# Biases of the query, key and value projection: from a matmul in each product to a shift of the weights

## The reference

```
x = x + attn(layernorm(x))        # 32 heads, 8 key/value heads, rope, causal, a sink per head
    qkv = n @ qkv_w.T + qkv_b     # 256 -> 3072
    ... softmax(q k / 8, with sink) @ v
    out @ out_w.T + out_b         # 2048 -> 256
x = x + xattn(layernorm(x), ctx)  # 8 heads over slices of the token axis
x = x + ffn(layernorm(x))         # top-1 of 8 experts, and a shared expert
```

## Time and profile before

| | us |
|---|---|
| median of 3 runs | 2182.62 |
| lowest and highest | 2179.29, 2183.5 |
| the profiled execution | 2175.44 |
| its span | 2173.4 |
| PE busy | 1990.2 (92%) |
| DVE busy | 1172.4 (54%) |
| ACT busy | 775.8 (36%) |
| POOL busy | 614.6 (28%) |
| granted clock of PE, mean | 0.978 |

### The profile page before, as it was taken

How to read it: one execution, slowest core, us unless ns; L and a number is a source line. 1 busy time by engine, 2 the same in 40 slices (tenths; PEclk the granted TensorE clock), 3 DMA queues, 4 the chain that set the end, 5 groups by cost and what they waited for, 6 DMA issues and landing times. The chain is left out here.

```text
span 2173.4 us, 49370 instructions
## 1 busy us (share of the span) xinstructions
PE 1990.2 (92%) x17680; PEld 1484.0 (68%) x17681; DVE 1172.4 (54%) x2333; ACT 775.8 (36%) x1463; POOL 614.6 (28%) x1100
## 2 busy tenths in 40 slices
PE   4999999999999999997799999999999599999998
PEld 3877787778777877786566666666666355666665
DVE  6566556655665566555566566666666122222221
ACT  3333333333333333333245444445455211211211
POOL 2232223222322232222222333332332310014443
PEclk9999999999999999999799999999999799999999
DMA  4011111111111111111323323323222155222221
GB/s 160 26 50 37 48 36 48 36 48 36 48 36 48 36 48 36 48 33 52 94 57 81 83 59 81 79 63 81 74 68 66 39 173 185 70 66 66 66 64 43
DMA packets 123545, 139.65 MB, mean 64 GB/s; under 512 B 16706, under 2 KB 118086, under 8 KB 121642
## 3 DMA queue, kind: packets, MB, share of 16 engines
q1 hardware_dynamic: 117674, 123.95, 20.3%
q0 software_dynamic: 5760, 14.06, 2.0%
HBM read 85.07 MB, written 53.52 MB: 64 GB/s over the span
## 5 line engine op out<-in xcount | busy, mean ns | idle before, releaser
L1032 ACT ACTIVATE xe<-bankXT 128x512 f32<-128x512 f32 x512 | 289.2, 596 | 324.8 <-PE bankXT L1173 317.8
L1073 DVE TENSOR_REDUCE xmax<-bankX 128x4 f32<-128x1024 f32 x256 | 309.2, 1210 | 133.5 <-PE bankX L1162 133.5
L1162 PE MATMUL bankX<-stk,stq 96*128 96x256 f32 x1024 | 230.7, 311 | 24.0 <-DMA rw<-in_rw 10.2
L543 DVE TENSOR_TENSOR oTl<-bankV,oTh 128x512 fp32r<-128x512 f32 x128 | 88.5, 691 | 303.9 <-ACT oTh L431 303.9
L1173 PE MATMUL bankXT<-stq,stk 98*128 98x256 f32 x1024 | 220.5, 298 | 6.7 <-ACT xe L1032 2.8
L1162 PEld LDWEIGHTS bankX<-stk,stq 96*128 96x128 f32 x1024 | 162.3, 198 | 55.5 <-issue 32.0
L649 PE MATMUL bankQ<-wqh,xnTh 128*128 128x512 f32 x384 | 188.5, 491 | 0.0
L1472 DVE TENSOR_TENSOR hid<-bankU,gate 128x512 f32<-128x512 f32 x72 | 49.8, 691 | 245.0 <-PE bankU L1525 241.9
L1173 PEld LDWEIGHTS bankXT<-stq,stk 98*128 98x128 f32 x1024 | 157.4, 191 | 32.0 <-ACT xe L1032 27.6
L360 POOL TENSOR_TENSOR prob<-prob,rden 128x1024 f32<-128x1024 f32 x64 | 121.9, 1905 | 170.5 <-DVE rden L539 170.5
L1188 PE MATMUL bankN<-xe,cT 128*32 128x256 f32 x2048 | 166.2, 397 | 0.2 <-ACT xe L1032 0.2
(11 more groups left out here) (177 smaller groups left out, 4090.2 us busy)
## 6 DMA issues: line engine op xcount, KB each, us to landing
stackk_d<-chl SPq DMA_DIRECT2D x96, 128.0 KB, 2.3
stackq_d<-q2hl SPq DMA_DIRECT2D x96, 128.0 KB, 2.3
stk<-stackk_d SPq DMA_DIRECT2D x32, 384.0 KB
stq<-stackq_d SPq DMA_DIRECT2D x128, 96.0 KB
wexp<-in_wexp SPq DMA_DIRECT2D x8, 1536.0 KB, 8.5
x_d<-x SPq DMA_DIRECT2D x64, 128.0 KB, 2.0
xin<-xg_d SPq DMA_DIRECT2D x40, 128.5 KB, 2.1
x<-in_x SPq DMA_DIRECT2D x32, 128.0 KB, 2.2
```

The lines of the kernel that those rows point to most:

```text
L543: nc.vector.tensor_tensor(oTl[g % 2][:], bV[:, 0, :].rearrange("p (a b) -> p a b", a=4), oTh[g % 2][:].bitcast(F32), ALU.subtract).then_in ...
L1032: nc.scalar.activation(xe[q % 8][:].rearrange("p n m -> p (n m)"), bT[:, q % 2, :], ACT.Exp).then_inc(s_xe, 1)
L1073: nc.vector.tensor_reduce(xmax[tile[1] % 2][:, :, a:b + 1:b - a].rearrange("p m h -> p h m"), bS[:, 2 * (pr % 2):2 * (pr % 2) + 2, :].rear ...
L1162: ins = nc.tensor.matmul(bS[:, q % 4, m * D:(m + 1) * D], stq[p][0:96, hd, m * P:(m + 1) * P], stk[p][0:96, hd // 4, :], start=True, stop= ...
```

## The change

The layer norm has no gain or bias, so each normalised row sums to zero. If 1 is added to each of its 256 entries, the product with a weight column grows by the sum of that column; if a constant is added to the whole weight column, the product with the row plus one grows by 256 times the constant. The weights are shifted by (bias - column sum) / 256, and the product of the row plus one with them is then the old product plus the bias. So no bias matmul is needed in `project`. The bias of the output projection stays a matmul.

- The row plus one: `turn_norm` on ACT uses Identity with bias 1.0 for Copy, and `turn_rest` on DVE a scalar_tensor_tensor (add 1.0, subtract the high part) for a subtraction.
- The column sums are formed on the chip. For each of the three pieces of the projection weight and each half of it, PE forms, in the bank of a product, minus the bias (bf16 matmul with `minusb`) plus the column sum (two float32 matmuls with `onesf`); DVE adds -1/256 of it to the raw weights (`fold`, 128 x 1024 elements, six times). Then ACT makes the high part and DVE the low part, as before.
- The output weights are in a buffer of their own (`stage_o`); their low parts are formed on POOL instead of DVE, and PE waits for them first in tile 1.
- The bias loads, the writes of the terms (two DMAs instead of six) and the read back are issued by ACT, ahead of its other work. SP no longer waits for them.
- Tiles 0 and 1 are normalised before the weights are folded.
- Waits and memsets are moved to fit, and the projection weight is laid out on the host in three pieces of 2 x 1024 columns.

```diff
@@ gpsimd, before the loop
+            for i in range(2):
+                pool.wait_ge(s_hio, i + 1)
+                nc.gpsimd.tensor_tensor(wlo[3 + i], raw[3 + i], whi[3 + i].bitcast(F32),
+                                        ALU.subtract).then_inc(s_loo, 1)
             nc.gpsimd.memset(G.stk0[:].bitcast(F32), 1.0)
@@ scalar
+            act.dma_start(bcol[:, 0:24], A["bqkv"].rearrange("(p c) -> p c", c=24)).then_inc(s_bias, 16)
+            act.dma_start(bcol[:, 24:26], A["bo"].rearrange("(p c) -> p c", c=2)).then_inc(s_bias, 16)
+            act.wait_ge(s_bterm, 1)
+            act.dma_start(G.bias_d[:, 0:3072].rearrange("k (p c) -> p k c", c=24), bterm[:, :, 0:24]).then_inc(s_brow, 16)
+            act.dma_start(G.bias_d[:, 3072:NBIAS].rearrange("k (p c) -> p k c", c=2), bterm[:, :, 24:26]).then_inc(s_brow, 16)
+            act.wait_ge(s_brow, 32)
+            act.wait_ge(s_setb, 1)
+            act.dma_start(bias3[0:3, :], G.bias_d).then_inc(s_brows, 16)
...
-                                     ACT.Copy).then_inc(s_xnTh, 1)
+                                     ACT.Identity, bias=1.0).then_inc(s_xnTh, 1)
...
             turn_norm((0, 0))
+            for i in (0, 1, 3, 2, 4):
+                high(i)
             tiles(act, body)
@@ vector
+            def fold(i, c):
+                dve.wait_ge(s_csum, 2 * i + c + 1)
+                part = raw[i][:, :, c * 512:(c + 1) * 512]
+                nc.vector.scalar_tensor_tensor(part, bk[c][:, 0, :].unsqueeze(1).to_broadcast([P, 2, 512]),
+                                               -1.0 / D, part, ALU.mult, ALU.add).then_inc(s_fold, 1)
+            def low(i):
+                dve.wait_ge(s_hi, i + 1)
+                nc.vector.tensor_tensor(wlo[i], raw[i], whi[i].bitcast(F32), ALU.subtract).then_inc(s_lo, 1)
...
+            stats1((0, 0))
+            norm1((0, 0))
+            stats1((0, 1))
+            turn_rest((0, 0))
+            norm1((0, 1))
...
+            for i in range(2):
+                for c in range(2):
+                    fold(i, c)
+            low(0)
+            for c in range(2):
+                fold(2, c)
+            low(1)
+            low(2)
@@ tensor
-                nc.tensor.matmul(out, onesb[:], bias3[:, col:col + 512], start=True, stop=False)
                 for k in range(2):
                     for n, (a, w) in enumerate(((xnTh, wqh), (xnTh, wql), (xnTl, wqh))):
-                        ins = nc.tensor.matmul(out, a[p][:, k, :], w[:, k, col:col + 512], start=False,
+                        ins = nc.tensor.matmul(out, a[p][:, k, :], w[:, k, col:col + 512], start=(k == 0 and n == 0),
                                                stop=(k == 1 and n == 2))
...
             turn_norm((0, 0))
+            pe.wait_ge(s_brows, 16)
+            pe.wait_ge(s_setb, 2)
+            for i in range(3):
+                pe.wait_ge(s_stage[i], 16)
+                for c in range(2):
+                    need(pe, s_fold, 2 * i + c - 1)
+                    col = i * 1024 + c * 512
+                    nc.tensor.matmul(bk[c][:, 0, :], minusb[:], bias3[:, col:col + 512], start=True, stop=False)
+                    for k in range(2):
+                        ins = nc.tensor.matmul(bk[c][:, 0, :], onesf[:], raw[i][:, k, c * 512:(c + 1) * 512],
+                                               start=False, stop=(k == 1))
+                    ins.then_inc(s_csum, 1)
             pe.wait_ge(s_setv, 1)
-            pe.wait_ge(s_brows, 16)
-            pe.wait_ge(s_lo, NSTAGE)
+            pe.wait_ge(s_setg, 2)
+            pe.wait_ge(s_lo, 3)
             tiles(pe, body)
```

More of the change, by code:

```diff
@@ L176, in attention @@
         NBIAS = 3072 + D
-        with nc.sbuf_tensor("stage", [P, NSTAGE, 2048], F32) as stage, \
+        stage_o = sb("stage_o", [P, 2, 2048])
+        with nc.sbuf_tensor("stage", [P, 3, 2048], F32) as stage, \
+                nc.sbuf_tensor("onesf_a", [P, P], F32) as onesf, \
+                nc.sbuf_tensor("minusb_a", [P, P], BF16) as minusb, \
                 nc.sbuf_tensor("bcol", [P, NBIAS // P], F32) as bcol, \
@@ L191, in attention @@
         s_stage = [sem(f"s_stage{i}") for i in range(NSTAGE)]
-        s_hi, s_lo = sem("s_hi"), sem("s_lo")
-        s_bias, s_setv, s_setg = sem("s_bias"), sem("s_setv"), sem("s_setg")
+        s_hi, s_hio, s_lo, s_loo = sem("s_hi"), sem("s_hio"), sem("s_lo"), sem("s_loo")
+        s_csum, s_fold = sem("s_csum"), sem("s_fold")
+        s_bias, s_setv, s_setg, s_setb = sem("s_bias"), sem("s_setv"), sem("s_setg"), sem("s_setb")
         s_bterm, s_brow, s_brows, c_bias, s_sinks = (
@@ L213, in attention @@
         s_q2hl, s_chl, g_c, g_q2 = sem("s_q2hl"), sem("s_chl"), sem("g_c"), sem("g_q2")
-        whi = [wqh[:].rearrange("p k n -> p (k n)")[:, i * 2048:(i + 1) * 2048] for i in range(3)] + [
+        whi = [wqh[:, :, i * 1024:(i + 1) * 1024] for i in range(3)] + [
             woh[:].rearrange("p k n -> p (k n)")[:, i * 2048:(i + 1) * 2048] for i in range(2)]
-        wlo = [wql[:].rearrange("p k n -> p (k n)")[:, i * 2048:(i + 1) * 2048] for i in range(3)] + [
+        wlo = [wql[:, :, i * 1024:(i + 1) * 1024] for i in range(3)] + [
             wol[:].rearrange("p k n -> p (k n)")[:, i * 2048:(i + 1) * 2048] for i in range(2)]
+        raw = [stage[:, i, :].rearrange("p (k n) -> p k n", k=2) for i in range(3)] + [
+            stage_o[:, i, :] for i in range(2)]
         wsrc = [A["wqkv"][:, i * 2048:(i + 1) * 2048] for i in range(3)] + [
@@ L247, in _ @@
                 sp.dma_start(x[p][:], A["x"][p * P:(p + 1) * P, :]).then_inc(s_x[p], 16)
-            sp.dma_start(bcol[:, 0:24], A["bqkv"].rearrange("(p c) -> p c", c=24)).then_inc(s_bias, 16)
-            sp.dma_start(bcol[:, 24:26], A["bo"].rearrange("(p c) -> p c", c=2)).then_inc(s_bias, 16)
             for i in range(NSTAGE):
-                sp.dma_start(stage[:, i, :], wsrc[i]).then_inc(s_stage[i], 16)
+                sp.dma_start(stage[:, i, :] if i < 3 else stage_o[:, i - 3, :], wsrc[i]).then_inc(s_stage[i], 16)
             sp.dma_start(sinks[:].rearrange("p r s -> p (r s)"),
                          A["sinks"].partition_broadcast(P)).then_inc(s_sinks, 16)
[L255 to L261, removed]
             sp.wait_ge(s_setg, 1)
@@ L313, in _ @@
             nc.gpsimd.memset(G.half[:], 0.5)
+            nc.gpsimd.memset(bias3[:], 0.0).then_inc(s_setb, 1)
+            nc.gpsimd.memset(half_neg[:], -0.5)
+            nc.gpsimd.memset(onesf[:], 1.0)
+            nc.gpsimd.memset(minusb[:], -1.0).then_inc(s_setb, 1)
             pool.wait_ge(s_const, 16)
             nc.gpsimd.tensor_copy(zeros[:, D:D + 1].bitcast(I32), C["none"]).then_inc(s_setg, 1)
-            nc.gpsimd.memset(half_neg[:], -0.5)
             nc.gpsimd.memset(onesb[:], 1.0)
-            nc.gpsimd.memset(bias3[:], 0.0)
             for p in range(2):
@@ L389, in _, with high @@
         def _(act):
-            for i in range(NSTAGE):
-                act.wait_ge(s_stage[i], 16)
-                nc.scalar.activation(whi[i], stage[:, i, :], ACT.Copy).then_inc(s_hi, 1)
+            act.dma_start(bcol[:, 0:24], A["bqkv"].rearrange("(p c) -> p c", c=24)).then_inc(s_bias, 16)
[6 more added lines that the diff above has]
+            act.dma_start(bias3[0:3, :], G.bias_d).then_inc(s_brows, 16)
+            def high(i):
+                if i < 3:
+                    act.wait_ge(s_fold, 2 * i + 2)
+                    nc.scalar.activation(whi[i], raw[i], ACT.Copy).then_inc(s_hi, 1)
+                else:
+                    act.wait_ge(s_stage[i], 16)
+                    nc.scalar.activation(whi[i], raw[i], ACT.Copy).then_inc(s_hio, 1)
             def turn_norm(tile):
@@ L472, in _ @@
         def _(dve):
-            dve.wait_ge(s_const, 16)
-            dve.wait_ge(s_setg, 2)
             def settle(tile):
@@ L501, in turn_rest @@
                 dve.wait_ge(s_xnTh, num(tile) + 1)
-                nc.vector.tensor_tensor(xnTl[tile[1]][:], bO[:, 0, D:2 * D].rearrange("p (k n) -> p k n", k=2),
-                                        xnTh[tile[1]][:].bitcast(F32), ALU.subtract).then_inc(s_xnT, 1)
+                nc.vector.scalar_tensor_tensor(xnTl[tile[1]][:], bO[:, 0, D:2 * D].rearrange("p (k n) -> p k n", k=2),
+                                               1.0, xnTh[tile[1]][:].bitcast(F32), ALU.add,
+                                               ALU.subtract).then_inc(s_xnT, 1)
             def rope(tile, c):
@@ L562, in _ @@
             ch.end()
[L563 to L566, removed]
+            stats1((0, 0))
[3 more added lines that the diff above has]
+            norm1((0, 1))
+            dve.wait_ge(s_const, 16)
+            nc.vector.tensor_copy(identb[:], ident)
+            nc.vector.tensor_copy(maskb[:], C["mask"])
+            nc.vector.tensor_copy(run[:], C["base"]).then_inc(s_setv, 1)
+            for i in range(2):
[6 more added lines that the diff above has]
+            low(2)
+            dve.wait_ge(s_setg, 2)
```

(5 more changed lines are left out.)

4 lines of the change are left out of this document (removed).

## The result

The changed kernel takes 2193.73 us (median of 8, 2189.19 to 2198.83), the kernel before 2180.14 (median of 8): a ratio of 1.0055, with a 95% interval from 1.0041 to 1.0068. By that ratio it is slower by 12 us (the medians lie 13.6 apart), where no measurable change with a lean to faster was forecast, and it lies outside the range. The profiled execution took 2195.25, its span is 2192.9, against 2173.4 before. The profiled execution of the kernel before (2175.44) is 4.7 us under that kernel's median, so spans taken from these two profiles lie further apart than the times do.

A forecast was written before the change was run, and what follows sets the result against it. Up to results(u, 0) DVE's chain with POOL and ACT was taken as the bound, then PE. Start +12.6, tile 0 -2.4, loop -13.3 gave -3.1 us: 2179.5, no measurable change with a lean to faster; range 2172.5 to 2186.

The forecast's parts named there:

- products 0, 1, 2: In the loop before turn_probs(u, 0): PE arrives 0.65 us earlier without their bias matmuls, prob no earlier; gain 0.
- product 3: In the loop between turn_probs(u, 0) and results(u, 0), where PE already waits: gain 0 from its bias matmul.
- Products 4 and 5: In the loop behind the last wait: gain 2 x 0.215, 0.43 us a tile in 31 tiles, 13.3 us.
- The longer stall: PE's wait before turn_probs(u, 0) in the loop: from 1.3 us to 1.7 to 2.0 a tile.
- The cover of product 5: In the loop, DVE's oTl for project_out(u, 2) stays hidden: 0.45 us of room against 0.215.
- Together 2.4: Tile 0 gets 2.4 us shorter: 1.5 for xn, 1.5 for six biases, 0.6 back for the lower clock.
- t0: At the start, the moment when the bias rows are in SBUF: taken as 20 us, bounds 15.9 and 27.7.
- t0 + 20.3: Start of tile 0: 17.3 us of column sums, folds and low parts plus a 3.0 us hold, at 40.3.
- the hold: At the start, POOL's subtraction of the output weights delays DVE's low(1): 3.0 us, bounds 0 and 6.8.
- the second as a rival: At the start, POOL's second subtraction also gets in before low(2): +3.8, giving +0.7 us, 2183.3; chance 0.14.
- The third one: At the start, bias rows no sooner than before, t0 27.7: +4.6 us or more, 2187.2; chance 0.12.
- Rivals 4 and 5: PE is the bound: -29.6, 2153.0, chance 0.05; longer stalls lower PE's clock in each tile: 2216.6, chance 0.05.

The follow-up runs named there:

- e9: The kernel before without the bias matmuls of products 0 to 3 only: 2180.86 us, ratio 0.9995 to the kernel before.
- e10: The kernel before without the bias matmuls of products 4 and 5 only: 2165.73 us, ratio 0.9924 to the kernel before.
- e3: The kernel before without the bias matmul of each product, nothing else changed: 2162.6 us, ratio 0.9921 to the kernel before.
- e2: The changed kernel with POOL's two output-weight subtractions begun only after DVE's three low parts: 2184.4 us, ratio 1.0018 to the kernel before.
- e7: The changed kernel with ACT's first evacuation of the turned probabilities before its second exponential: 2167.85 us, ratio 0.9940 to the kernel before.
- e1: The changed kernel with SP's eight zero writes held back until the bias rows are in SBUF: 2185.3 us, ratio 1.0021 to the kernel before.
- e4: The changed kernel with SP's weight loads and all behind them held back until the bias rows are in SBUF: 2185.89 us, ratio 1.0028.
- e13: The changed kernel with zero writes behind the bias rows and POOL's subtractions behind DVE's low parts: 2177.78 us, ratio 0.9980.
- e8: The changed kernel with one-DMA float32 bias row, POOL's subtractions behind DVE's low parts, and loop reordered on DVE, POOL and ACT: 2117.61 us, ratio 0.9711.
- e14: The changed kernel with one-DMA float32 bias row and POOL's subtractions behind DVE's low parts, loop unchanged: 2165.33 us, ratio 0.9925.
- e5: The changed kernel with the projection bias loaded as one float32 row in one DMA, bf16 terms only for the output bias: 2172.38 us, ratio 0.9957.

## Why the prediction was wrong

- **The loop: right.** "That is 0.43 us a tile in the 31 tiles with a rear part": 0.42 measured. "products 0, 1, 2 [...] Gain 0" and "product 3 [...] Gain 0": e9 measured 0.9995 without all four. Products 4 and 5 carry it all: e10. The number for products 4 and 5 isn't luck: from the last matmul ahead of it to its own end, product 4 takes 0.21 us less in the tiles shown (1.51 instead of 1.72), and from the start of the `results` ahead of it product 5 takes 0.22 less (2.25 instead of 2.47). The longer stall was forecast at 1.7 to 2.0 us and is 1.53, because part of it moved ahead of `turn_probs(u, 0)`, to `turn_qk(tile, 0)` (4.2 us in 24 tiles) and `scores(u, 1)` (2.0 in 11); the wait before `results` grew by about what product 3 lost (0.25). The cover of product 5 held. The changed evacuation on DVE takes 0.41 as before.
- **Tile 0: nearly right, in part by luck.** "Together 2.4": 3.1 up to `turn_norm` of tile 2. e3, e9 and e10 show that this number also depends on when PE's clock rises: there `turn_norm` of tile 2 came 1.0 to 1.6 us later than in the kernel before, from a start at most 0.6 later and with fewer matmuls.
- **The failed step: t0.** "I take 20: the queue is another one, the engines are the same full ones", with an upper bound of 27.7 ("they still wait for the loads"). It was 36.5: the second write was issued at 8.38 instead of 6.5, landed 22.3 us later, and the read back took 5.8 instead of 2.2. The same code had the rows at 35.0 in the profile of e2 and at 33.0 in that of e7, so some 3 us of it vary from one execution to the next; all three are above the bound. Two things stood behind that bound. The first is that the zero writes, which SP no longer holds back, were taken for something that comes after the small writes. They come beside them: between 20 and 31 us the engines are full at 70 GB/s (e1: 9.6 us of t0, with the loads that stand behind the zeros held back too). The second is that the 7.2 us after the loads were taken for the tail of 768 writes alike, where in the changed kernel they are the 4-byte ones: in e1 the 48-byte DMA landed 11.0 us after its issue at 7.62, with the loads, the 4-byte one at 24.5; by themselves they take 2.2 and 9.1 us (e4), and a wait for both DMAs is a wait for the second. In the kernel before the two kinds were issued in turn, and no run separates them there. The upper bound was no bound, since it assumed that nothing else would change on the queues.
- **t0 + 20.3 was t0 + 28.4.** 5.0 of that are the hold: both low parts, 12.6 us against 7.6. I had it at one hold and priced the second as a rival (0.14); the row chosen for it had one POOL operation after another too, and one DVE operation waited for both there. Here DVE got its turn between POOL's two, and each of its own two waited for one (e2). 2.9 are the column sums: 1.93 us from one to the next at the upper clock, where I worked out 1.1. Each float32 matmul of 512 columns stands twice in the trace at 0.43; the group of four in the earlier trace rows belongs to two matmuls of the program. The last 0.2 lie between the end of the last low part and PE's first matmul.
- **The rivals.** The third one was the right side and mechanism, with too small a price: "+4.6 us or more, 2187.2", measured 2193.7; it came together with the second. Rivals 4 and 5 are out: PE isn't the bound up to `results` (e9), and the clock is 1.00 from 100 to 1000 us.
- **The sum.** In the two profiles it is +37.2 - 17.7 = +19.5 us of span, forecast +12.6 - 15.7 = -3.1. Of the 24.6 us between 64.95 and 40.3, 16.5 are t0, 5.0 the hold and 2.9 the column sums. The times differ by 12 us and not by 19.5. From the last `turn_norm` of the loop to the end, the profiles with the changed kernel's loop have 1220.6 to 1225.0 us (1223.2 in its own), those of the kernel before and of e9, whose tiles lie as far apart, 1225.7 and 1229.1. So a sum over two single profiles is good to some us only, and the times decide. e13 takes back 18.2 us of start and, by the times, the sign of the result.

## What to carry to other kernels

A matmul that lay in front of a wait on another engine's chain cost nothing here, and taking it out gained nothing: read which engine works without a gap up to the wait, count the matmuls behind the last wait alone, and shorten that chain first (two statements moved on DVE and one on POOL gave 35 us here, 192 matmuls taken out gave 17). When a wait is taken off a queue, everything behind it on that queue starts sooner and beside what used to have the engines to itself; price that, and give the upper bound of a landing with it. Look in each group of small DMAs for the one with the smallest elements and ask whether it has to be waited for there.

## What was not expected of the hardware

- A DMA of 384 elements of 4 bytes to DRAM lands after 9.1 us with nothing beside it, one of 384 elements of 48 bytes after 2.2 (e4).
- With 1 MB of writes of 1028-byte rows and some loads beside the 4-byte ones, the DMA engines were 1.10 busy at 70 GB/s for 11 us. In e1, where the 4-byte ones had landed before, they moved 178 GB/s at 0.97 between 31 and 37 us.
- DVE subtractions with both operands in SBUF (2.24 us each) and POOL's of the same kind don't run beside each other: two of DVE's took 12.61 us beside two of POOL's, 4.48 without (e2). They took turns, operation by operation.
- After 10 us without work and one `turn_norm`, PE reached its upper clock level some 5 us into the column sums in e8 and e14 and some 17 us into them in e5, by the durations of its matmuls; the code is the same up to there.
